# Four stacked transformer blocks on one core: which heads get their added mask on VectorE and which on TensorE

## The reference

```python
logits = jnp.einsum('bqhd,bkhd->bhqk', q, k)      # head size 16, 512 x 512
logits = logits + mask[:ql, :kl]                  # mask_SxS_fc0, any values
p = jax.nn.softmax(logits, axis=-1)
o = jnp.einsum('bhqk,bkhd->bqhd', p, v)
```

## Time and profile before

| what | us |
|---|---|
| median of 3 runs | 4814.16 |
| lowest, highest | 4795.39, 4820.23 |
| the profiled execution | 4813.37 |
| its span, first to last instruction | 4811.6 |
| the stage with the added mask, in it | about 2141 to 2912 |
| granted TensorE clock, mean | 0.928 of 2.4 GHz |

### The profile page before, as it was taken

The page is one execution under the profiler, slowest core; times in us unless marked ns, Lnnn a source line. Parts: engine busy times, 40 slices in busy tenths (PEclk is TensorE's granted clock), DMA queues, the critical chain, the costliest instruction groups (busy, mean ns, idle before and its releaser), DMA issues. The chain is left out here.

```text
span 4811.6 us, 76408 instructions
## 1 busy us (share of the span) xinstructions
PE 4392.0 (91%) x22610; PEld 2202.8 (46%) x22610; DVE 2706.3 (56%) x6114; ACT 2289.0 (48%) x4789; POOL 1240.8 (26%) x1277
## 2 busy tenths in 40 slices
PE   5999999889896889899999999999899799999998
PEld 3555543333464333334444443333366455555555
DVE  3555677776102777787766767777400344444443
ACT  2444456555221556554444446665422355454553
POOL 1111111111221111111111111111022566666664
PEclk9888899998797889999999999998799899999999
DMA  4433434333001443433222223434100000000000
GB/s 106 64 55 59 69 73 77 66 62 59 16 0 23 89 73 62 72 58 63 47 46 46 43 47 77 81 61 74 33 16 0 27 5 10 10 10 10 10 6 10
DMA packets 115381, 218.33 MB, mean 45 GB/s; under 512 B 22320, under 2 KB 25008, under 8 KB 113328
## 3 DMA queue, kind: packets, MB, share of 16 engines
q1 hardware_dynamic: 114992, 213.79, 24.2%
HBM read 39.11 MB, written 4.19 MB: 9 GB/s over the span
## 5 line engine op out<-in xcount | busy, mean ns | idle before, releaser
L907 ACT ACTIVATE Pr<-ST 128x512 f32<-128x512 f32 (+3 forms) x2560 | 1359.1, 564 | 1370.8 <-PE ST L492 1069.9
L1089 DVE TENSOR_REDUCE mx<-MX 128x1 f32<-128x512 f32 (+3 forms) x1408 | 855.0, 629 | 503.8 <-PE MX L492 468.2
L492 PE MATMUL ST<-stk 50*128 50x512 f32 (+3 forms) x2560 | 1115.5, 486 | 16.5 <-ACT Pr L907 13.9
L492 PE MATMUL MX<-stk 48*128 48x512 f32 (+3 forms) x1760 | 773.5, 475 | 165.1 <-DMA stk<-lo 87.4
L492 PE MATMUL OV<-Pr,V 128*32 128x512 f32 (+3 forms) x5120 | 710.4, 630 | 1.5 <-ACT Pr L907 1.5
L492 PEld LDWEIGHTS MX<-stk 48*128 48x128 f32 x1760 | 329.3, 199 | 781.1 <-DVE mx L1089 414.2
L1408 POOL TENSOR_SCALAR Pr<-Pr,mx 128x128 f32<-128x128 f32 (+3 forms) x512 | 548.4, 1083 | 385.4 <-DVE mx L1227 385.4
L492 PEld LDWEIGHTS ST<-stk 50*128 50x128 f32 x2560 | 461.1, 199 | 139.7 <-ACT Pr L907 108.9
L1089 DVE TENSOR_REDUCE mx<-OV 128x1 f32<-128x512 f32 (+3 forms) x640 | 399.9, 625 | 136.3 <-PE OV L492 135.9
L1342 POOL CAST mhl<-mx 128x16 fp32r<-128x16 f32 x160 | 31.9, 199 | 1464.3 <-DVE mx L1089 1110.0
L1339 POOL TENSOR_TENSOR X<-X,brow 128x1024 f32 (+1 forms) x56 | 132.3, 2363 | 1014.7 <-DVE X L1041 1014.7
(11 more groups left out here) (134 smaller groups left out, 6766.7 us busy)
## 6 DMA issues: line engine op xcount, KB each, us to landing
stk<-hi SPq DMA_DIRECT2D x640, 128.0 KB, 3.9
stk<-lo SPq DMA_DIRECT2D x320, 128.0 KB, 4.0
misc<-misc SPq DMA_DIRECT2D x160, 128.0 KB, 3.8
sums<-misc SPq DMA_DIRECT2D x160, 128.0 KB, 4.0
misc<-in_ctx_t SPq DMA_DIRECT2D x24, 512.0 KB, 4.9
W_even<-in_w SPq DMA_DIRECT2D x4, 1024.0 KB, 5.6
W_even<-in_w SPq DMA_DIRECT2D x2, 2048.0 KB, 7.8
XH<-in_ctx_rows SPq DMA_DIRECT2D x8, 512.0 KB, 4.2
```

The lines of the kernel that those rows point to most:

```text
L492: return nc.tensor.matmul(o, l, r, start=start, stop=stop)
L907: nc.scalar.activation(Pr[:, i % 2, h, q0:S], ST[h % 2][:, q0:S], ACT.Exp).then_inc(ex_done, 1)
L1089: nc.vector.tensor_reduce(m, bank[:, 0:k_n], AX.X, ALU.max).then_inc(mx_red, 1)
```

## The change

Head 2 of each four moves from the identity products to VectorE. VectorE now adds the mask to heads 0 and 2, TensorE to 1 and 3. ScalarE's wait for the added mask counts two adds a step in place of one. Nothing else is changed; `add_mask` and `score_tile` read the tuple.

```diff
-        MASKED_BY_PE = (1, 2, 3)
+        MASKED_BY_PE = (1, 3)
...
                     if addmask and h not in MASKED_BY_PE:
-                        act.wait_ge(st_masked, 8 * u + i + 1)
+                        act.wait_ge(st_masked, 2 * (8 * u + i) + h // 2 + 1)
                     else:
                         act.wait_ge(st_full, at + 1)
```

## The result

| | before | after |
|---|---|---|
| median of 10 runs each, us | 4804.32 | 4849.62 |
| lowest, highest | 4787.89, 4820.23 | 4825.23, 4864.44 |
| span of the profiled execution | 4811.6 | 4835.8 |
| mean granted clock | 0.928 | 0.915 |

The ratio is 1.0100, with an interval of 1.0079 to 1.0121: the change makes the kernel 1% slower, about 45 us. That lies inside the range (4770 to 4852), at its upper end. It is not the forecast of 4812.

A forecast was written before the change was run, and what follows sets the result against it. TensorE was taken to bound the masked stage (764.5 of 771 us). Long steps' savings were eaten by stretched short steps: -0.1 us a pair, about -1 over eight pairs, so 4813.4 - 1 = 4812 us; range 4770 to 4852.

The forecast's parts named there:

- The loop of 5.30 us: Masked stage: short steps, without other TensorE work, cannot average under 5.30 us through VectorE's add; 5.03 now.
- Rivals A and B: Masked stage: A, all 85 us saved, 4728, chance 0.07; B, short steps keep length, 24 at most, 4789, chance 0.15.
- The sum of a pair, -0.1: Masked stage: step changes of an even and an odd slot, 8 steps each, sum to -0.1 us.
- Even 5: Step 5 of an even slot, with a 1.8 us TensorE job behind score h3: 0.57 us saved, length near 6.0.
- odd 1 and 2: Steps of an odd slot: 1 saves 0.57 us but loses 0.3 to the emptied product bank; 2 changes by -0.1.
- Odd 4: Step 4 of an odd slot: VectorE's queued reciprocals delay h2's maximum and exp, +0.9 us, from 6.16 to near 7.
- even 4: Step 4 of an even slot: score h3 waits for exp h1 behind the activation of `hT`; nothing saved, 0.
- VectorE's room: Masked stage: 83 us of adds on 541 make 624, 81% of today's stage, so VectorE fits as a sum.
- Rival C: Masked stage: TensorE's clock falls in short steps, 6.8 us a fall, 41 us for six pairs: 4853, chance 0.20.
- The row from 3190: Profile row with TensorE busy 8.33 of 10 us at granted clock 1.00, cited against Rival C.
- The row from 2620: Masked stage: profile row busy 7.97 of 10 us, granted 0.67, the next 0.65; priced a fall at 6.8 us.
- No DMA, queue or load moves: Whole change: 256 products go, 128 adds come, and no DMA, queue or load moves; no time was assigned.

The follow-up runs named there:

- (2): Changed kernel with VectorE adding head 2's mask ahead of its maximum, not behind it: 4783.62 us, ratio 0.9959 to before.
- (3): Kernel before, with head 2 on VectorE only in 40 of 128 steps, the long ones: 4778.64 us, ratio 0.9970 to before.
- (4): Kernel before with head 2's identity pair removed and no add in its place, so head 2 gets no mask: 4733.88 us, ratio 0.9864.
- The filling pair: Changed kernel with one more identity pair for head 3 in the short steps, adding that mask twice: 4812.72 us, ratio 1.0033 to before.
- (7): 136 already met VectorE waits added behind the masked stage's loop: to before 1.0042, to the changed kernel 1.0083; also to two other variants, 1.0017 and 0.9848.

## Why the prediction was wrong where it was

- **The loop of 5.30 us: right.** 5.24 to 5.26 measured, each link within 0.05 us; with 0.62 taken from it the short steps came down to 4.6 to 4.7 (2). Rivals A and B fall with it: the short steps did stretch.
- **The sum of a pair, -0.1: right in kind, 0.8 too high.** Fifteen steps are within 0.35 us. Even 5 was predicted at 6.1 and took 6.93. Its score h3 came when predicted (+3.16 for +3.20), but the projection behind it waits 0.7 us for VectorE's low part, which now stands behind the add of h2 (the lines in 3). The prediction had no term for that. It is not the add of step 4: with that left to TensorE the step takes 6.93 all the same (3). Against it fourteen others came out 0.03 to 0.32 shorter than given, odd 1 and 2 most. Odd 4 (+0.9 predicted, +0.7 measured) and even 4 (0, +0.07) were as read. The stage at a steady clock: -7 us for -1.
- **VectorE's room: right.** 604 us for the predicted 624, and 76% of the stage for 81%, since an add cost less and the stage grew. TensorE's share is 94% for the forecast 88%, because its matmuls took longer at the lower clock: with the same matmuls at 0.99 it is busy for 681 us (4), 88% of 771.
- **Rival C, at a chance of 0.20: it was this.** The step that failed is "The row from 3190 does not bear it out". One slice of 10 us in another stage, with TensorE busy 8.33 of 10 at 1.00, stood for eight short steps in a row, and so the sum had no term for the clock. The row from 2620, the fall in this very stage, was no measure either: it holds one stop of 2.0 us, not eight small waits. No row of before shows such a run of steps. The stage is 23 to 34 us longer than the step lengths allow (26.5 + 7 in the first pair of profiles, 15.7 + 7 in the second: what the stage grew, and the 7 that the steps should have given back), while what the clock lacks adds up to 58 us more than before; the rest may be hidden in steps where TensorE waits anyway, which is argued and not shown. Rival C's 6.8 us a fall and six more falls had given 41. The filling pair brings the clock to 0.99 and the stage to 759, so the clock as the cause of the longer stage is shown, not argued. The rule of the Trainium skill that the prediction weighed (TensorE: Matmul & The Clock Gate, A second HAM failure mode) agrees: the score waits are at most 1.2 us, TensorE stands still for over 1 us three times only, and the clock falls in all eight pairs.
- **"No DMA, queue or load moves": true of the work, not of the program.** No step of the prediction had a term for the 17 to 19 us of the next stage, and this is the second step that failed. Instructions added or taken move the programs of VectorE and TensorE, and a loop behind the edit ran differently, with VectorE stopping where it waits for nothing (7). The old stops of 3 us stood in the trace of before.
- The terms together: 7 less than before by the steps, 23 to 34 by the clock, 17 to 19 by the next stage: 33 to 45 us, for the measured 45 of the medians. The spans of the same two pairs of profiles differ by 24 and 13, because of the part ahead of the stage. That the time fell inside the range is partly luck: the range reached up there for rival C, but 17 to 19 of the 45 us came from a stage that the prediction had left out.

Open: what exactly starts a fall; which placement of the program is bad; whether the next stage's lower clock (0.87) follows from its stops or has a cause of its own; what before gains from h0's add ahead of its maximum alone.

## What to carry to other kernels

When TensorE bounds only some of the steps, work handed to another engine pays in these alone, and in the others it can close a loop through that engine; write down the loop's links, then ask which operation on it could stand behind the one that feeds the next engine (here the add of h2 ahead of its maximum turned +1% into -0.4%; with h0's add ahead as well and step 4 left to TensorE it was -1.4%). Give the granted clock a term of its own when many steps in a row leave TensorE waiting a little, and check that a row used as its price shows such waits and not one long stop. After any edit, compare the stages that it did not touch: if one has moved, look there for "issue" stops.

## What the runs showed that I had not expected

- 136 waits of VectorE that do nothing took 23 us out of a stage behind them (571 to 548), while the stage that holds them took 6 us more; the same 136 in before put 7 us in.
- More matmuls made the stage shorter: 143 more records, 39 us less, by the clock alone.
- With both adds ahead of their maxima the stage (691 us) is shorter than with head 2's mask left out altogether in the old order (700 us).
